# Local attention of the last sub-layer, rebuilt on four tiles per pass with one PSUM region for each function

## The chip, the core and the metric

The kernel runs on one core of a Trainium2 chip. The metric is the device time of one launch in microseconds (us), from the first to the last instruction and what little lies around it. Five engines work side by side, each through a list of its own in order: PE (matrix multiply, with its weight loads shown as PEld), DVE (VectorE), ACT (ScalarE), POOL (GpSimd) and SP (which issues DMAs). They wait for each other by semaphores only.

## The reference

Eight sub-layers are added to `x` (128 sequences of 64 tokens, width 128) one after another. The last one has two layers, each with a local attention (the part that is changed) and a gated GELU block. For one layer of the attention, with 8 heads of 64 and a window of 64 over sequences of 64 tokens (so one causal block for each sequence):

```python
h = shift_token(x)                      # second half of the columns comes from the token before
q, k, v = split(h @ wqkv)               # 8 heads of 64 each
q = l2norm(q) * qs ; k = l2norm(k) * ksc
q = q * cos * scale + rotate_half(q) * sin * scale
k = k * cos / scale + rotate_half(k) * sin / scale
attn = softmax(8.0 * q @ k.T  + causal mask)
x = x + (attn @ v) @ wo
```

## The kernel before

All of the program is a chain of stages, and every stage ends with a barrier of all engines. `X` and, in the last sub-layer, `y` (`l3f_y`) stay in SBUF: 64 tiles of 128 rows, where a tile holds two sequences of 64 tokens. `local_attention` runs twice (stages `la0`, `la1`), each time over the 64 tiles, as a software pipeline: the helper `steps` writes two steps (tile j = 0, 1) into the body of a loop, and `at(it, j, lag, work)` puts a function on the tile that lies `lag` tiles ahead. Within an engine the order is the order of the `at` lines; between engines only semaphores count. Every buffer exists twice (j).

PSUM has four regions of two banks each: `m.A[0]`, `m.A[1]`, `m.B[0]`, `m.B[1]`. Tile j uses `A[j]` (banks `F0`, `F1`) for h, q, k, v and the turned q and k, and `B[j]` (banks `G0`, `G1`) for scores, turned probabilities, mixed values and the projection.

The steps of one tile, with the lines of the profile:

- ACT copies the rows (L1942), PE turns them and shifts by a token with the `shift` matrix (`turn_y`, L2107 and L2108), ACT copies hT (L1947, L1949).
- PE makes q and k (`make_qk`, L2115, L2116), ACT squares them out of PSUM (L1955, L1956), DVE sums per head (`lengths`, L2003) and floors (L2006).
- POOL raises the sums to the power -0.5 (L2089). DVE multiplies q and k by it out of PSUM (`normalize`, L2012). POOL makes the two sine halves (L2095, L2096), DVE the cosine part (`cosines`, L2020), POOL adds them (L2099) into `la_qk`.
- PE makes v in the banks that q and k leave (`make_v`, L2121), ACT keeps v spread out with zeros (`values`, L1925); PE turns `la_qk` (`turn_qk`, L2130), and ACT and DVE copy q and k out, k spread out with zeros (L1967, L1930).
- PE makes the scores of 8 heads with a mask matmul (L2135) and 8 matmuls of 64x128 (`scores`, L2141); DVE takes the maxima and subtracts (`shift`, L2031, L2034); ACT takes the exponential (L1972); PE turns (L2151), ACT copies (L1977), PE mixes with v and a column of ones (`mix`, L2160), DVE divides (`outputs`, L2043, L2048), PE turns (L2168), ACT copies (L1982), PE projects (`project`, L2174), DVE adds to y (`add`, L2056).

Of the kernel before, what the change touches and what calls it, by code (L numbers as in the profile page):

```python
# [16 lines left out]
S = 64  # L17
# [1866 lines left out]

def local_attention(nc, m, d, y, layer):
# [3 lines left out]
    with Stage(nc, f"la{layer}") as st:  # L1889
# [4 lines left out]
        half_power = st.sb("half_power", [P, 2 * HEADS3])  # L1894
# [3 lines left out]
        ys, hT, hT2 = st.two("ys", [P, P]), st.two("hT", [P, P]), st.two("hT2", [P, 2, 2, S])  # L1898
        sq, qk, turned = (st.two(n, [P, 2, INNER]) for n in ("sq", "qk", "turned"))
        length, rlen = st.two("length", [P, 2 * HEADS3]), st.two("rlen", [P, 2 * HEADS3])  # L1900
        qT = st.two("qT", [P, G, P])
        kd = st.two("kd", [P, G, 2, 2, S])
        vd = st.two("vd", [P, 2, G, 2, W3 + 1])
        prob, pT = st.two("prob", [P, HEADS3, S]), st.two("pT", [P, G, P])
        top, inv = st.two("top", [P, HEADS3]), st.two("inv", [P, HEADS3])
        o, oT = st.two("o", [P, INNER]), st.two("oT", [P, G, P])
        loaded, ready, ones_set = st.sem("loaded"), st.sem("ready"), st.sem("ones_set")
        (y_copied, y_turned, h_copied, qk_made, squared, summed, floored, rooted, scaled, v_made, v_kept,
         cosed, sined, rotated, qk_turned, q_copied, k_kept_low, k_kept_high, scored, max_done,
         shifted, exped, p_turned, p_copied, mixed, inverted, o_done, o_turned, o_copied, out_done, added) = (  # L1910
            st.sem2(n) for n in ("y_copied", "y_turned", "h_copied", "qk_made", "squared", "summed", "floored",
                                 "rooted", "scaled", "v_made", "v_kept", "cosed", "sined",
                                 "rotated", "qk_turned", "q_copied", "k_kept_low", "k_kept_high", "scored",
                                 "max_done", "shifted", "exped", "p_turned", "p_copied", "mixed", "inverted",
                                 "o_done", "o_turned", "o_copied", "out_done", "added"))

        F0, F1 = [x[:, 0:CH] for x in m.A], [x[:, CH:2 * CH] for x in m.A]
        G0, G1 = [x[:, 0:CH] for x in m.B], [x[:, CH:2 * CH] for x in m.B]
        blocks = lambda x: x.rearrange("p (g q) -> p g q", g=G)

        def keep_v(eng_copy, j, u):

            r = slice(u * S, u * S + S)
            for b, src in enumerate((F0[j], F1[j])):
                last = eng_copy(vd[j][r, b, :, u, 0:W3], src.rearrange("p (g u w) -> p g u w", g=G, u=2)[r, :, u])  # L1925
            return last

        def keep_k(eng_copy, j, u):
            r = slice(u * S, u * S + S)
            return eng_copy(kd[j][r, :, :, u], F1[j].rearrange("p (g b k) -> p g b k", g=G, b=2)[r])  # L1930

        with nc.Block() as block:
# [4 lines left out]

            @block.scalar
            def _(act):
                def copy_y(it, j):  # L1940
                    act.wait_ge(y_turned[j], past(it))
                    act.copy(ys[j][:], y[:, it * 2 + j, :]).then_inc(y_copied[j], 1)  # L1942

                def copy_h(it, j):
                    act.wait_ge(y_turned[j], past(it + 1))
                    act.wait_ge(v_made[j], past(it))
                    act.copy(hT[j][:], F0[j][:, 0:P])  # L1947
                    for b in range(2):
                        last = act.copy(hT2[j][:, b], repeat_heads(F0[j][:, b * S:b * S + S], 2))  # L1949
                    last.then_inc(h_copied[j], 1)  # L1950

                def squares(it, j):
                    act.wait_ge(qk_made[j], past(it + 1))
                    act.wait_ge(rotated[j], past(it))
                    act.activation(sq[j][:, 0], F0[j], ACT.Square)  # L1955
                    act.activation(sq[j][:, 1], F1[j], ACT.Square).then_inc(squared[j], 1)  # L1956

                def values(it, j):
                    act.wait_ge(v_made[j], past(it + 1))
                    act.wait_ge(mixed[j], past(it))  # L1960
                    keep_v(act.copy, j, 0)
                    keep_v(act.copy, j, 1).then_inc(v_kept[j], 1)

                def copy_qk(it, j):
                    act.wait_ge(qk_turned[j], past(it + 1))
                    act.wait_ge(scored[j], past(it))
                    act.copy(qT[j][:], blocks(F0[j])).then_inc(q_copied[j], 1)  # L1967
                    keep_k(act.copy, j, 1).then_inc(k_kept_high[j], 1)

                def exps(it, j):  # L1970
                    act.wait_ge(shifted[j], past(it + 1))
                    act.activation(prob[j][:], prob[j][:], ACT.Exp, scale=8.0).then_inc(exped[j], 1)  # L1972

                def copy_p(it, j):
                    act.wait_ge(p_turned[j], past(it + 1))
                    act.wait_ge(mixed[j], past(it))
                    act.copy(pT[j][:], blocks(G1[j])).then_inc(p_copied[j], 1)  # L1977
# [17 lines left out]

                steps(act, step)

            @block.vector
            def _(dve):
                def lengths(it, j):  # L2000
                    dve.wait_ge(squared[j], past(it + 1))
                    dve.wait_ge(rooted[j], past(it))
                    dve.tensor_reduce(length[j][:], sq[j][:].rearrange("p n (h w) -> p (n h) w", h=HEADS3), AX,  # L2003
                                      ALU.add).then_inc(summed[j], 1)
                    dve.wait_ge(summed[j], past(it + 1))
                    dve.tensor_scalar(length[j][:], length[j][:], 1e-24, None, ALU.max).then_inc(floored[j], 1)  # L2006

                def normalize(it, j):
                    dve.wait_ge(rooted[j], past(it + 1))
                    dve.wait_ge(qk_turned[j], past(it))  # L2010
# [547 lines left out]
```

## Time and profile before

| | us |
|---|---|
| median of three runs | 5108.8 (5107.85 to 5109.19) |
| profiled execution, its own time | 5109.92 |
| its span, first to last instruction | 5108.1 |
| PE busy over the span | 4115.2 (81%) |
| DVE busy | 3229.7 (63%) |
| ACT busy | 2027.8 (40%) |
| POOL busy | 1890.4 (37%) |

The two attention stages are two of some twenty stages. Each of them goes through 64 tiles at an even pace, so they are best read as one tile's pace times 64 plus what the beginning and the end take. In the rows below, a line of the timeline gives the start, the duration (of a merged group: from the first start to the last end), the engine, the line, the operation with output and inputs, how many records it has, and in brackets how long the engine had been idle and what released it. A group line of the profile gives the busy time, the mean of one instruction in ns, and the idle time before. An fp32 matmul shows two records, a transpose one.

### The profile page before, as it was taken

Reading aid. Unit: us, or ns where it says so; the run is one execution under the profiler, and the core shown is the slowest. Engines: PE = TensorE matmul, PEld = TensorE weight load, DVE = VectorE, ACT = ScalarE, POOL = GpSimd, SP = SyncE. Lnnn points to the kernel's source line nnn. Section 1 sums busy time; section 2 is a strip of 40 time slices with the busy share of each in tenths; the row PEclk is TensorE's granted clock in tenths of the full one; section 3 lists DMA queues with packets and bytes.
Section 4 is the critical chain, followed back from the end, with each engine's and each line's share of the span. In section 5 each row is a group of like instructions: output and inputs, shape, how many; then the busy total and the mean of one; then the engine's idle time right before and its main releaser. Section 6 shows DMA issues by size and latency. Waiting matters only on the chain. (4 is left out here: it accounts for less than half of the span.)

```text
span 5108.1 us, 83277 instructions
## 1 busy us (share of the span) xinstructions
PE 4115.2 (81%) x25803; PEld 2577.4 (50%) x25803; DVE 3229.7 (63%) x6921; ACT 2027.8 (40%) x4429; POOL 1890.4 (37%) x1457
## 2 busy tenths in 40 slices
PE   6772899998995850469959979699898889989987
PEld 5441444445773320346646656355555445555544
DVE  3998301106776698857767755577776447777744
ACT  1332222224663154334422236455555225555521
POOL 0775000002330054135510000288887018888810
PEclk9996899999996975789959975699999989999999
DMA  2110000000000000021100020000000000000000
GB/s 75 41 40 13 23 0 0 0 0 13 11 11 7 0 0 0 0 60 35 35 14 0 0 75 8 11 0 0 0 0 0 5 11 0 0 0 0 0 5 33
DMA packets 76953, 67.34 MB, mean 13 GB/s; under 512 B 11988, under 2 KB 72536, under 8 KB 75736
## 3 DMA queue, kind: packets, MB, share of 16 engines
q1 hardware_dynamic: 75448, 66.23, 4.3%
q8 instruction: 29, 0.48, 0.0%
q10 hardware_dynamic: 1440, 0.34, 0.0%
q14 instruction: 36, 0.29, 0.0%
HBM read 62.34 MB, written 4.19 MB: 13 GB/s over the span
## 5 line engine op out<-in xcount | busy, mean ns | idle before, releaser
L2089 POOL TENSOR_TENSOR la_rlen<-la_length,la_half_power 128x16 f32<-128x16 f32 x128 | 372.8, 2912 | 55.6 <-DVE la_length L2006 48.8
L2099 POOL TENSOR_TENSOR la_qk<-la_turned,la_sq 128x1024 f32<-128x1024 f32 x128 | 301.2, 2353 | 46.7 <-DVE la_turned L2020 39.2
L750 DVE TENSOR_TENSOR l0f_y<-A,l0f_s 128x512 f32<-128x512 f32 x16 | 11.1, 692 | 463.4 <-PE A L717 463.4
L2096 POOL TENSOR_TENSOR la_sq<-la_qk,la_sin 128x512 f32<-128x512 f32 x128 | 259.7, 2029 | 0.0
L2121 PE MATMUL A<-la_wv,la_hT 128*128 128x512 f32 x512 | 257.3, 625 | 1.4 <-DVE la_qk L2012 1.4
L2012 DVE TENSOR_TENSOR la_qk<-A,la_rlen 128x512 f32<-128x512 f32 x256 | 164.9, 687 | 145.2 <-POOL la_rlen L2089 145.2
L1925 ACT COPY la_vd<-A 64x256 f32<-64x256 f32 x512 | 163.6, 369 | 228.5 <-PE A L2121 227.1
L2130 PE MATMUL A<-ident,la_qk 128*128 128x128 f32 x1024 | 137.3, 277 | 136.1 <-ACT la_vd L1925 87.2
L2082 POOL COPY la_vd<-half 128x8 f32<-128x8 f32 x8 | 1.2, 198 | 657.1 <-POOLq L47 657.1
L1006 POOL COPY l1x_vd<-half 128x16 f32<-128x16 f32 x4 | 0.6, 213 | 650.6 <-POOLq L47 650.6
L1869 PE MATMUL A<-l1f_wT,l1f_down_oq 128*128 128x128 f32 x384 | 54.2, 307 | 226.0 <-DVE l1f_down_oq L1830 225.9
L2095 POOL TENSOR_TENSOR la_sq<-la_qk,la_sin 128x512 f32<-128x512 f32 x128 | 163.8, 1280 | 179.4 <-DVE la_qk L2012 179.4
L1015 POOL TENSOR_TENSOR l1x_kx<-l1x_kT,head_of 128x512 f32<-128x512 f32 x128 | 130.8, 1043 | 263.2 <-ACT l1x_kT L1116 263.2
L2130 PEld LDWEIGHTS A<-ident,la_qk 128*128 128x128 f32 x1024 | 110.4, 141 | 166.8 <-POOL la_qk L2099 164.5
L1972 ACT ACTIVATE la_prob<-la_prob 128x512 f32<-128x512 f32 x128 | 81.0, 633 | 285.7 <-DVE la_prob L2034 285.7
L2020 DVE TENSOR_TENSOR la_turned<-la_qk,la_cos 128x1024 f32<-128x1024 f32 x128 | 189.4, 1479 | 0.1
L1930 DVE COPY la_kd<-A 64x512 f32<-64x512 f32 x128 | 87.4, 683 | 150.8 <-PE A L2130 150.8
L2303 ACT ACTIVATE gg_gate<-B,gg_b 128x512 f32<-128x512 f32 (+1 forms) x96 | 65.9, 686 | 280.0 <-PE B L2334 280.0
L1869 PEld LDWEIGHTS A<-l1f_wT,l1f_down_oq 128*128 128x128 f32 x384 | 51.3, 218 | 230.2 <-DVE l1f_down_oq L1830 215.1
L2003 DVE TENSOR_REDUCE la_length<-la_sq 128x16 f32<-128x1024 f32 x128 | 154.8, 1209 | 14.3 <-ACT la_sq L1956 14.3
L2160 PEld LDWEIGHTS B<-la_vd,la_pT 128*64 128x64 f32 x2048 | 111.1, 136 | 92.8 <-issue 92.5
L2291 POOL TENSOR_TENSOR gg_rstd<-gg_var,gg_half_power 128x4 f32<-128x4 f32 x32 | 32.3, 1009 | 335.5 <-DVE gg_var L2248 335.5
(442 smaller groups left out, 11947.5 us busy)
## 6 DMA issues: line engine op xcount, KB each, us to landing
memory_ctx<-in_ctx SPq DMA_DIRECT2D x128, 64.0 KB, 2.2
l2x_ctx<-in_ctx SPq DMA_DIRECT2D x128, 64.0 KB, 2.2
X<-in_x SPq DMA_DIRECT2D x4, 1024.0 KB, 8.7
gates_ctxT<-in_ctxT SPq DMA_DIRECT2D x16, 256.0 KB, 2.7
memory_ctxT<-in_ctxT SPq DMA_DIRECT2D x64, 64.0 KB, 1.7
l1x_ctxT<-in_ctxT SPq DMA_DIRECT2D x64, 64.0 KB, 1.7
l2x_raw<-in_l2x_mask SPq DMA_DIRECT2D x2, 2048.0 KB
l2x_ctxT<-in_ctxT SPq DMA_DIRECT2D x64, 64.0 KB, 1.7
```

Of the source, the lines that this page charges most:

```text
L1015: last = pool.tensor_tensor(kx[j][:, b], repeat_heads(k_in[j][:, b * S:b * S + S], E), spread_heads(m.head_of_8[:], S), ALU.mult)
L1925: last = eng_copy(vd[j][r, b, :, u, 0:W3], src.rearrange("p (g u w) -> p g u w", g=G, u=2)[r, :, u])
L2003: dve.tensor_reduce(length[j][:], sq[j][:].rearrange("p n (h w) -> p (n h) w", h=HEADS3), AX, ALU.add).then_inc(summed[j], 1)
L2012: last = dve.tensor_tensor(per_head(qk[j][:, n], HEADS3, W3), per_head(src, HEADS3, W3), spread_heads(rlen[j][:, n * HEADS3:(n + 1) * HEAD ...
L2020: dve.tensor_tensor(heads(turned[j][:]), heads(qk[j][:]), cos[:, :, None, :].broadcast_to([P, 2, HEADS3, W3]), ALU.mult)\
L2089: pool.tensor_tensor(rlen[j][:], length[j][:], half_power[:], ALU.pow).then_inc(rooted[j], 1)
L2095: pool.tensor_tensor(z[:, :, :, lo], x[:, :, :, hi], along(lo), ALU.mult)
L2096: pool.tensor_tensor(z[:, :, :, hi], x[:, :, :, lo], along(hi), ALU.mult).then_inc(sined[j], 1)
L2099: pool.tensor_tensor(qk[j][:], turned[j][:], sq[j][:], ALU.add).then_inc(rotated[j], 1)
L2121: last = pe.matmul(dst, hT2[j][:, b].rearrange("p u k -> p (u k)"), wv[:], start=True, stop=True)
L2130: last = pe.transpose(dst[:, g * P:g * P + P], qk[j][:, n, g * P:g * P + P], m.ident[:])
L2160: last = pe.matmul(dst[b * S:b * S + S, g % 2 * n:g % 2 * n + n], pT[j][:, g, b * S:b * S + S], vd[j][:, b, g].rearrange("p u w -> p (u w) ...
```

## The change

`local_attention` is written anew. The rest of the program is the same.

- Four tiles per loop body instead of two (`steps4`, `at4`), one counting semaphore for each event (`done(it, j, back)` is the count at which tile `it*4+j-back` has done it).
- PSUM regions by function, each used by every tile in turn: `made` (q and k), `keyed` (turned q and k; then turned h in its upper bank and v in its lower one), `tried` (scores and turned probabilities), `used` (mixed values; then turned outputs and projection).
- The shifted rows come by DMA from `y` into `hs` (three DMAs a tile, issued by SP), and one transpose turns them (`turn_h`).
- q and k are not normalized first: DVE multiplies the raw q and k out of PSUM by cosine and sine (`cosines`, `sine_terms`), POOL adds (`rotate`) and then scales by the inverse length (`scale`).
- The inverse length is Exp(-0.5 * Ln(65536 * length)) on ACT (`root`) instead of a power on POOL; the factor is undone by 256 in the tables. POOL floors the sums (`floor`).
- Scores, mix and v use tiles of 64 columns: 16 matmuls of 64x64 for the scores, 16 of 64x65 for the mix, 4 of 64x256 for v. The copies with zeros between (`kd`, `vd`) go.
- q and k are copied in one ACT copy of 1024 columns, v in one of 512, the squares are one ACTIVATE of 1024.

The core of the diff (old parts of `local_attention` that only fall away are in the listing above):

```diff
+def at4(it, j, lag, work, quads=QUADS):
+    quad, j = it + (j + lag) // 4, (j + lag) % 4
...
+        made, keyed, tried, used = m.A[0], m.A[1], m.B[0], m.B[1]
+        sim = banks(tried)[:, :, 0:G * S].rearrange("p u (g k) -> p u g k", g=G)
+        turned_p = banks(tried)[:, :, G * S:CH]
+        turned_o, projected = used[:, 0:CH], used[:, CH:CH + P]
+        turned_h, made_v = keyed[:, CH:CH + P], keyed[:, 0:CH]
...
+                def shift_in(it, j):
+                    sp.wait_ge(h_turned, done(it, j, 4))
+                    sp.dma_start(hs[j][:, 0:S], y[:, t, 0:S]).then_inc(h_in[j], 16)
+                    for b in range(0, P, S):
+                        sp.dma_start(hs[j][b + 1:b + S, S:P], y[b:b + S - 1, t, S:P]).then_inc(h_in[j], 16)
...
             @block.scalar
+                def copy_qk(it, j):
+                    act.wait_ge(qk_turned, done(it, j))
+                    act.wait_ge(scored, done(it, j, 2))
+                    act.copy(qkT[j % 2][:].rearrange("p n g q -> p (n g q)"), keyed[:]).then_inc(qk_copied, 1)
+                def root(it, j):
+                    act.wait_ge(floored, done(it, j))
+                    act.wait_ge(scaled_qk, done(it, j, 2))
+                    act.activation(rlen[j % 2][:], length[j % 2][:], ACT.Ln, scale=65536.0).then_inc(logged, 1)
+                    act.wait_ge(logged, done(it, j))
+                    act.activation(rlen[j % 2][:], rlen[j % 2][:], ACT.Exp, scale=-0.5).then_inc(rooted, 1)
...
+                def values(it, j):
+                    act.wait_ge(v_made, done(it, j))
...
-                    at(it, j, 2, copy_y)
-                    at(it, j, 0, copy_qk)
-                    at(it, j, -1, copy_p)
-                    at(it, j, 2, copy_h)
-                    at(it, j, 0, exps)
-                    at(it, j, 2, squares)
-                    at(it, j, 1, values)
-                    at(it, j, -1, copy_o)
+                    at4(it, j, 0, copy_qk)
+                    at4(it, j, -1, copy_p)
+                    at4(it, j, -2, copy_o)
+                    at4(it, j, 0, exps)
+                    at4(it, j, 1, values)
+                    at4(it, j, 3, squares)
+                    at4(it, j, 4, copy_h)
+                    at4(it, j, 2, root)
             @block.vector
+                    at4(it, j, 2, cosines)
+                    at4(it, j, 2, sine_terms)
+                    at4(it, j, 0, shift)
+                    at4(it, j, 2, lengths)
+                    at4(it, j, -2, add)
+                    at4(it, j, -1, outputs)
             @block.gpsimd
+                    at4(it, j, 1, scale)
+                    at4(it, j, 2, rotate)
+                    at4(it, j, 2, floor)
             @block.tensor
+                def turn_qk(it, j):
+                    pe.wait_ge(scaled_qk, done(it, j))
+                    pe.wait_ge(v_kept, done(it, j))
+                    pe.wait_ge(h_copied, done(it, j, -3) if not isinstance(it, int) else min(done(it, j, -3), NT + BEFORE))
+                def scores(it, j):
+                    pe.wait_ge(p_copied, done(it, j, 1))
+                    pe.matmul(banks(tried)[:, 0, 0:G * S], m.ident_bf[:], repeat_heads(m.causal_bf[:], G),
+                              start=True, stop=False)
+                    pe.wait_ge(qk_copied, done(it, j))
+                    pe.matmul(banks(tried)[:, 1, 0:G * S], m.ident_bf[:], repeat_heads(m.causal_bf[:], G),
+                              start=True, stop=False)
+                    for g in range(G):
+                        for b in range(2):
+                            for u in range(2):
+                                r, c = slice(u * S, u * S + S), slice(b * S, b * S + S)
+                                last = pe.matmul(sim[c, u, g], qkT[j % 2][r, 0, g, c], qkT[j % 2][r, 1, g, c],
+                                                 start=False, stop=(g == G - 1))
+                def make_v(it, j):
+                    pe.wait_ge(qk_copied, done(it, j, 1))
```

The order of the instructions on two engines in the loop bodies. ACT before, the first of the two tiles of the body: `la_qT` and the first `la_kd` are the turned q and k, `la_sq` the squares.

```order
L1942 COPY la_ys<-l3f_y 128x128
L1967 COPY la_qT<-A 128x512
L1930 COPY la_kd<-A 64x8x64
L1977 COPY la_pT<-B 128x512
L1945 REGISTER_ALU
L1947 COPY la_hT<-A 128x128
L1949 COPY la_hT<-A 128x128 x2
L1972 ACTIVATE la_prob<-la_prob 128x512
L1955 ACTIVATE la_sq<-A 128x512
L1956 ACTIVATE la_sq<-A 128x512
L1925 COPY la_vd<-A 64x4x64 x4
L1982 COPY la_oT<-B 128x512
```

There is no table load in the loop. ACT in the changed kernel, from the copy of h (`la_hT`) through `root` (`la_rlen`) to the values of the next step:

```order
L2015 COPY la_hT<-A 128x128
L1986 REGISTER_ALU
L1988 ACT_TABLE_LOAD
L1988 ACTIVATE la_rlen<-la_length 128x16
L1990 ACT_TABLE_LOAD
L1990 ACTIVATE la_rlen<-la_rlen 128x16
L1982 REGISTER_ALU
L1983 COPY la_qkT<-A 128x1024
L1995 COPY la_pT<-B 128x512
L2000 COPY la_oT<-B 128x512
L2004 ACTIVATE la_prob<-la_prob 128x512
L2009 COPY la_vd<-A 128x8x64
```

The logarithm (L1988) and the exponential (L1990) of `root` have each got a table load, eight in the body of four tiles, and the copies of a tile stand behind them.

PE before, one tile of the body (`A` and `B` are the PSUM regions, `la_wv` the weights of v):

```order
L2130 MATMUL A<-ident,la_qk 128x128 x8
L2151 MATMUL B<-ident,la_prob 128x128 x4
L2174 MATMUL B<-la_wo,la_oT 128x128 x4
L2107 MATMUL A<-ident,la_ys 64x128
L2108 MATMUL A<-shift,la_ys 64x128
L2135 MATMUL B<-causal_bf,ident_bf 128x512
L2141 MATMUL B<-la_kd,la_qT 64x128 x8
L2115 MATMUL A<-la_wq,la_hT 128x512
L2116 MATMUL A<-la_wk,la_hT 128x512
L2160 MATMUL B<-la_vd,la_pT 64x130 x8
L2121 MATMUL A<-la_wv,la_hT 128x512 x2
L2168 MATMUL B<-ident,la_o 128x128 x4
```

PE in the changed kernel, from the masks of a tile's scores to the end of its step:

```order
L2160 MATMUL B<-causal_bf,ident_bf 128x256
L2163 MATMUL B<-causal_bf,ident_bf 128x256
L2169 MATMUL B<-la_qkT 64x64 x16
L2153 REGISTER_ALU
L2154 REGISTER_ALU
L2155 MATMUL A<-la_wq,la_hT 128x512
L2156 MATMUL A<-la_wk,la_hT 128x512
L2176 MATMUL B<-la_wo,la_oT 128x128 x4
L2181 REGISTER_ALU
L2182 MATMUL A<-ident,la_hs 128x128
L2188 MATMUL A<-la_wv,la_hT 64x256 x4
L2203 MATMUL B<-la_vd,la_pT 64x65 x16
```

The matmuls of v (L2188) now stand behind the scores (L2169), q and k of a later tile (L2155, L2156) and the projection (L2176); before, they stood behind the mix, and waited for the normalized q and k.

On POOL the power (L2089) and both sine halves (L2095, L2096) are gone, the sum stays, and the scaling (1024 columns) and the floor (16 columns) are new.

## Rows read from the trace of the kernel before

**Rows 1.** Busy time in stretches: us, PE, PEld, DVE, ACT, POOL (records), clock, DMA share.

```profile
3600.00:3809.00 209.00, 188.63 (x1382) 121.58 (x1381) 157.18 (x260) 118.58 (x301) 170.68 (x81) 1.00 0.00 0
150.00:200.00 50.00, 38.56 (x417) 24.09 (x416) 45.55 (x104) 16.22 (x42) 39.75 (x52) 1.00 0.15 41
3100.00:3150.00 50.00, 45.85 (x195) 32.13 (x194) 30.05 (x131) 32.46 (x132) 0.00 (x0) 0.50 0.00 0
```

**Rows 2.** Timeline of one tile of la0 on POOL and DVE; the last row: a tile later.

```profile
3598.80 2.92 POOL L2089 TENSOR_TENSOR la_rlen<-la_length,la_half_power 128x16 f32<-128x16 f32 x1
...
3601.75 1.29 DVE L2012 TENSOR_TENSOR la_qk<-A,la_rlen 128x512 f32<-128x512 f32 x2 [1.05 <-POOL la_rlen L2089]
...
3603.11 1.26 POOL L2095 TENSOR_TENSOR la_sq<-la_qk,la_sin 128x512 f32<-128x512 f32 x1 [1.40 <-DVE la_qk L2012]
...
3604.33 2.32 POOL L2096 TENSOR_TENSOR la_sq<-la_qk,la_sin 128x512 f32<-128x512 f32 x1
...
3606.73 2.35 POOL L2099 TENSOR_TENSOR la_qk<-la_turned,la_sq 128x1024 f32<-128x1024 f32 x1
...
3609.28 2.91 POOL L2089 TENSOR_TENSOR la_rlen<-la_length,la_half_power 128x16 f32<-128x16 f32 x1 [0.19 <-DVE la_length L2006]
```

**Rows 3.** The same timeline, the maxima of two tiles that follow each other.

```profile
3602.98 0.69 DVE L2031 TENSOR_REDUCE la_top<-B 128x8 f32<-128x512 f32 x1
...
3613.43 0.69 DVE L2031 TENSOR_REDUCE la_top<-B 128x8 f32<-128x512 f32 x1
```

**Rows 4.** The same timeline: PE from the projection of a tile to the values.

```profile
3600.16 1.06 PE L2174 MATMUL B<-la_wo,la_oT 128*128 128x128 f32 x8
...
3601.52 0.39 PE L2135 MATMUL B<-causal_bf,ident_bf 128*128 128x512 bf16 x1
...
3601.84 1.09 PE L2141 MATMUL B<-la_kd,la_qT 128*64 128x128 f32 x16
...
3602.86 1.12 PE L2115 MATMUL A<-la_wq,la_hT 128*128 128x512 f32 x2
...
3605.82 1.98 PE L2121 MATMUL A<-la_wv,la_hT 128*128 128x512 f32 x4
...
3607.64 0.60 PE L2168 MATMUL B<-ident,la_o 128*128 128x128 f32 x4
...
3607.84 1.29 ACT L1925 COPY la_vd<-A 64x256 f32<-64x256 f32 x4 [1.80 <-PE A L2121]
...
3609.27 1.06 PE L2130 MATMUL A<-ident,la_qk 128*128 128x128 f32 x8 [1.03 <-ACT la_vd L1925]
```

**Rows 5.** Groups of instructions on ACT: busy us, mean ns of one, idle before.

```profile
L1137 ACT COPY l1x_pT<-A 128x1024 f32<-128x1024 f32 x64 | 64.8, 1012 | 39.4 <-PE A L1197 39.4
L1972 ACT ACTIVATE la_prob<-la_prob 128x512 f32<-128x512 f32 x128 | 81.0, 633 | 285.7 <-DVE la_prob L2034 285.7
L1956 ACT ACTIVATE la_sq<-A 128x512 f32<-128x512 f32 x128 | 75.4, 589 | 0.0
L1977 ACT COPY la_pT<-B 128x512 f32<-128x512 f32 x128 | 75.0, 586 | 3.1
L1947 ACT COPY la_hT<-A 128x128 f32<-128x128 f32 x128 | 34.1, 266 | 15.4 <-PE A L2108 15.4
L409 ACT ACTIVATE memory_low<-memory_low 128x8 f32<-128x8 f32 x64 | 12.8, 200 | 0.6
```

**Rows 6.** Timeline of ACT where an exponential and a logarithm follow each other.

```profile
103.86 0.63 ACT L290 ACTIVATE decay_l<-decay_f 128x512 f32<-128x512 f32 x1
104.51 1.28 ACT L292 ACT_TABLE_LOAD   x1
105.80 0.63 ACT L292 ACTIVATE decay_l<-decay_l 128x512 f32<-128x512 f32 x1
```

**Rows 7.** Timeline of PE in the l2x stage, 64-column tiles with 18 moving columns.

```profile
2500.99 1.11 PE L1208 MATMUL B<-l2x_vd,l2x_pT 128*64 128x18 f32 x32 [0.16 <-ACT l2x_pT L1137]
```

**Rows 8.** Groups of instructions on DVE, same columns as Rows 5.

```profile
L1051 DVE TENSOR_TENSOR l1x_prob<-A,l1x_top 128x1024 f32<-128x1024 f32 x64 | 78.4, 1225 | 2.2
L2003 DVE TENSOR_REDUCE la_length<-la_sq 128x16 f32<-128x1024 f32 x128 | 154.8, 1209 | 14.3 <-ACT la_sq L1956 14.3
```

**Rows 9.** Timeline of PE at the start of la1.

```profile
4180.72 0.47 PE L2107 MATMUL A<-ident,la_ys 128*64 128x128 f32 x1 [12.46 <-DMA la_by_swapped<-in_l3f_scale_swapped]
...
4182.12 2.08 PE L2115 MATMUL A<-la_wq,la_hT 128*128 128x512 f32 x2 [0.70 <-ACT la_hT L1949]
```

**Rows 10.** The adds to y in both layers: duration min/median/max, first and last start.

```profile
L2056 DVE TENSOR_TENSOR l3f_y<-l3f_y,B x128: 272/275/289, 3316.4 to 4873.2; 128x128 f32 x120, 128x128 f32<-128x128 f32 x8
```

More of the change, by code:

```diff
@@ L1882, with done, steps4 @@
 PARTS3 = [(n, min(P, HID3 - n)) for n in range(0, HID3, P)]
+QUADS = NT // 4
+BEFORE = 4
+def done(it, j, back=0):
+    return it * 4 + j + 1 + BEFORE - back
+def at4(it, j, lag, work, quads=QUADS):
+    quad, j = it + (j + lag) // 4, (j + lag) % 4
+    if not isinstance(quad, int) or 0 <= quad < quads:
+        work(quad, j)
+def steps4(eng, step, quads=QUADS):
+    for it in (-1, 0):
+        for j in range(4):
+            step(it, j)
+    with eng.Fori(1, quads - 1) as it:
+        for j in range(4):
+            step(it, j)
+    for it in (quads - 1, quads):
+        for j in range(4):
+            step(it, j)
 def local_attention(nc, m, d, y, layer):
@@ L1917, in local_attention @@
[L1917 to L1930, printed above, removed]
+        qkT = st.two("qkT", [P, 2, G, P])
@@ L1938, in _ @@
+                steps4(sp, step)
             @block.scalar
             def _(act):
-                def copy_y(it, j):
-                    act.wait_ge(y_turned[j], past(it))
-                    act.copy(ys[j][:], y[:, it * 2 + j, :]).then_inc(y_copied[j], 1)
-                def copy_h(it, j):
[L1945 to L1950, printed above, removed]
@@ L1964, in copy_qk @@
[L1964 to L1977, printed above, removed]
@@ L1998, in _ @@
+                    at4(it, j, 2, root)
+                steps4(act, step)
             @block.vector
             def _(dve):
-                def lengths(it, j):
[L2001 to L2006, printed above, removed]
@@ L2053, in add, with cosines @@
-                def add(it, j):
-                    t = it * 2 + j
-                    dve.wait_ge(out_done[j], past(it + 1))
-                    dve.tensor_tensor(y[:, t, :], y[:, t, :], G1[j][:, 0:P], ALU.add).then_inc(added[j], 1)
-                for j in range(2):
-                    dve.memset(kd[j][:], 0.0).then_inc(ones_set, 1)
-                    dve.memset(vd[j][:, :, :, :, 0:W3], 0.0).then_inc(ones_set, 1)
+                def cosines(it, j):
+                    dve.wait_ge(squared, done(it, j))
+                    dve.wait_ge(scaled_qk, done(it, j, 2))
+                    dve.tensor_tensor(heads(turned[j % 2][:]), made_heads,
+                                      cos[:, :, None, :].broadcast_to([P, 2, HEADS3, W3]), ALU.mult)\
+                       .then_inc(cosed, 1)
@@ new lines, in turn_p, with turn_o @@
+                def turn_p(it, j):
+                    pe.wait_ge(exped, done(it, j))
+                    for g in range(G):
+                        last = pe.transpose(turned_p[:, g // 2, g % 2 * P:g % 2 * P + P],
+                                            prob[j % 2][:, g].rearrange("p u k -> p (u k)"), m.ident[:])
+                    last.then_inc(p_turned, 1)
+                def turn_o(it, j):
+                    pe.wait_ge(o_done, done(it, j))
+                    for g in range(G):
+                        last = pe.transpose(turned_o[:, g * P:g * P + P], o[j % 2][:, g * P:g * P + P], m.ident[:])
+                    last.then_inc(o_turned, 1)
@@ new lines, in scores, with project, turn_h @@
+                    last.then_inc(scored, 1)
+                def project(it, j):
+                    pe.wait_ge(o_copied, done(it, j))
+                    for g in range(G):
+                        last = pe.matmul(projected, oT[j % 2][:, g], wo[:, g], start=(g == 0), stop=(g == G - 1))
+                    last.then_inc(out_done, 1)
+                def turn_h(it, j):
+                    pe.wait_ge(h_in[j], it * 48 + 48)
+                    pe.wait_ge(qk_copied, done(it, j, 4))
+                    pe.transpose(turned_h, hs[j][:], m.ident[:]).then_inc(h_turned, 1)
@@ L2177, in _ @@
+                    last.then_inc(mixed, 1)
                 pe.wait_ge(loaded, 16 * len(loads))
```

297 lines of the change are left out of this document (131 added, 166 removed).

## The prediction

> **What bounds the kernel now.** I read the stretches first [rows 1]: in steady attention (3600 to 3809 us) PE is busy 90%, POOL 82%, DVE 75%, ACT 57%, at a granted clock of 1.00 (2.4 GHz). None is full, so a loop through several engines sets the pace. The timeline shows it [rows 2]: power 2.92 on POOL, then `normalize` on DVE 1.29 (POOL idle for 1.40), the sine halves 1.26 and 2.32, the sum 2.35, a gap of 0.19, and the next power. Together 10.4, and the maxima of two tiles lie 10.45 us apart [rows 3]. That is the pace P of before; 64 tiles in each of two layers make 1338 us. The rest of the program is the same, so each us of P is worth 128 us.
>
> **What goes.** The whole POOL loop. DVE now needs nothing from POOL to read q and k, and POOL has two passes of 1024 columns at 2.35 and a floor of 16 columns: bounded below by about 0.2 and above by the power's 2.9 [rows 2], so 4.9 to 7.6 a tile. DVE: cosines out of PSUM 1.23 and sums 1.21 (1024 columns, [rows 8]), the sine halves 2 x 0.65 as `normalize` [rows 2], maxima 0.69 [rows 3], the subtraction as much, some 1.1 for division and add: 6.2. Neither sets a pace near 10.
>
> **What comes: one loop through ACT and PE.** The table of the order decides here. In a step ACT does copy q and k of t, copy p of t-1, copy o of t-2, exponential of t, values of t+1, squares of t+3, h of t+4, root of t+2. The values of t+1 wait for `make_v` of t+1, which on PE stands behind the scores of t, q and k of t+3, the projection of t-2 and the turned h. The scores of t wait for the copy of p of t-1, since `tried` exists once. So nothing of this overlaps within a tile's pace, and I add it up from the start of copy_qk (running sum in brackets):
>
> - ACT: copy of 1024 columns 1.01 and of 512 columns 0.59 [rows 5], and 0.02 behind each (1.62).
> - ACT to PE 0.14: the values' copy ends at 3609.13, the transpose starts at 3609.27 [rows 4] (1.76).
> - Masks to the first score 0.32 as before: 3601.52 to 3601.84; 512 bf16 columns stay 512 (2.08).
> - Scores: 16 matmuls, 32 records. Before, 16 records of 128 moving columns took 1.02 to the start of the next group, of which 0.86 is eight pairs at 0.107 and 0.16 the way out [rows 4]. With few columns a record of a 64-column tile takes (1.11 - 0.21) / 31 = 0.029, a pair 0.058 [rows 7]; that is 0.93 for 16 pairs, 0.46 if four go together, 1.70 if the two row halves go one after another (32 x 0.053). No row shows tiles of 64 rows. I take 0.60, nearer to four together, since the row halves write different banks and share nothing; with the way out 0.76 (2.84).
> - q and k of t+3: four records of 512 columns, as the values' four from 3605.82 to 3607.64: 1.82 (4.66).
> - Projection: eight records at (1.06 - 0.275) / 7 = 0.112: 0.90 (5.56). Turned h: 0.11 (5.67).
> - Values: 0.10 for the change of tile size, then eight records of 256 columns in four pairs, 0.213 each (half of 0.427), the last ending 0.17 later and the first 0.05 slower: 1.07 (6.84). If the pairs do not overlap, 0.85 more.
> - PE to ACT 0.04; the copy of v 0.59, squares 0.589 + 512 x 0.833 ns = 1.02, h 0.27 [rows 5], 0.02 behind each (8.82).
> - Root: two table loads at 1.283 (1.28 in [rows 6]), two ACTIVATEs of 16 columns at 0.20 (128x8, [rows 5]), four times 0.02: 3.05 (11.87).
>
> Then copy_qk of the next tile starts: its transposes wait only for h (at 8.82), take PE 0.14 + 1.03, and are there at 10.0; those of p at 10.6. So they are hidden, by 1.2 us; without the table loads they would be next, and the gain from leaving these out would end near 1.4.
>
> What lies beside this loop: the subtraction of t ends near 4.4 and the exponential near 5.1, both before the values at 6.88. POOL scales t+1 from 0 and is done with the sum near 4.9; the sums of DVE come near 5.6, the floor by 6.0 to 8.7, needed at 8.8 at the earliest. The DMAs of h run up to four tiles ahead, some 45 us, and cost PE no wait; if that cover went, a wait of a few us would stand in front of the turned h. The copies with zeros and the copies of y cost nothing before either (they lay in ACT's idle 43%), so their going brings nothing. I take the mix, 16 of 64x65, at the scores' 0.76; it stands behind the values in PE's idle time.
>
> So P goes from 10.45 to 11.87. The bounds: scores at 0.46 and no extra for tile sizes (0.26 less) 11.47; scores at 1.70 12.97. Beginning and end of a layer take 24 us before (4180.7 to 4873.5 less 64 x 10.45, [rows 9, 10]), partly at half clock (q's two records 2.08 instead of 1.12, [rows 4, 9]). Two more tiles in flight add some, fewer semaphores to set at the start take a little: +6, between -5 and +15. **Sum:** 2 x (64 x 1.42 + 6) = 194. Against the profiled execution's own 5109.9 (span 5108.1 and 1.8 around it; 1.1 over the median) that is 5304.
>
> **Two pages weighed against the rows.** Where an exponential is followed by a logarithm in the trace, the load starts 0.02 after the ACTIVATE ends and the next ACTIVATE 0.01 after the load [rows 6]: a switch costs 1.29. The Trainium skill ("ScalarE: Activation LUTs", What ACT_TABLE_LOAD costs) gives 1283 ns for the load plus about 1380 ns of drain at each switch; the trace shows no such drain, and by that rule P would be an estimated 2.76 longer (14.63, 5657). The Trainium skill, same page, section "Table sets: the hidden batching unit", says that exponential and logarithm share a set and need one load; by this an estimated 1.3 would fall away, 5137, but the program as built has both loads in the loop body, so this gets no chance. The Trainium skill, "TensorEngine Tiling (Array Packing)", Key Properties, says that different tiles run weight loads and matmuls in parallel, and that a change of the tiling mode drains TensorE. The drain agrees with the rows (0.10 to 0.16 at each change, [rows 4]); on four tiles at once no run here speaks, and by this rule alone the scores would be 0.46, P 11.73 and the time 5286.
>
> **The rivals.**
> - *The loop does not close, and the busiest engine sets the pace (faster).* This would need PE to have `make_v` done before ACT wants it. ACT's own sum is 1.03 + 0.61 + 0.61 + 0.65 + 0.61 + 1.04 + 0.29 + 3.05 = 7.89, and 3.98 of P is idle before exponential and values. The sign turns where this idle time is below 10.45 - 7.89 = 2.56. At nothing, P is 7.9 and the time 5110 - 2 x (64 x 2.55 - 6) = 4796. For it: PE's whole work is some 7.5. Against: both queues are in order, and the wait of the scores for the copies is in the same step.
> - *The row halves go one after another.* P 12.97, 5445.
> - *The clock falls.* PE's share falls from 90% to some 65%. At half clock (1.2 GHz) the PE part of the loop (1.76 to 6.84) adds 5.1: P 17, near 5960. For it: the l3x stage ran throughout at 0.50. Against: the memory stage, with PE busy 77%, kept 1.00 [rows 1].
> - *Each load empties ACT first.* If ACT stood idle at each load for as long as the load itself takes (1.28), P would be 11.87 + 2.57 = 14.44 and the time 5110 + 2 x (64 x 3.99 + 6) = 5633. Against: the 0.02 and 0.01 around the load in [rows 6].
> - *Nothing changes.* The new loop would happen to be 10.3 to 10.4 long.
>
> **The chances.** The forecast has 0.73, serial row halves 0.08, half clock 0.08, drains 0.04, the faster case 0.05, no change 0.02. The likeliest is 5304. The range takes the bounds of the scores, the tile changes and the ends: low 2 x (64 x 1.02 - 5) above 5110, that is 5230, opened to 5220; high the serial case with the ends at +15, 5463. It leaves out half clock, drains and the faster cases, some 0.19. A measurement here can tell 0.2% (10 us) from no change: faster 0.05, same 0.02, slower 0.93.
>
> **What would show it.** Maxima (DVE) 11.9 us apart; two table loads of 1283 ns for each tile, 256 in all; ACT idle about 2.2 before the exponential (released by DVE) and 1.8 before the values (released by PE); PE idle before the scores some 3 us a tile, released by ACT; DVE and POOL far from full, POOL's passes 2.35 or less; clock 1.00. The step on the scores is read off as the distance from the first score to the next q: 0.76. I am wrong if ACT does not wait for the values, if the pace is set by DVE or POOL, or if the clock is below 1.00 in the steady part.

## The result, and the profile after

| | before | after |
|---|---|---|
| median of four runs, us | 5108.96 (5107.85 to 5109.19) | 5302.32 (5301.92 to 5303.88) |
| span of the profiled execution | 5108.1 | 5300.5 |
| mean granted clock of TensorE | 0.899 | 0.883 |
| from first to last maxima, la0 and la1 | 659.2 and 659.4 | 752.1 and 752.1 |

The ratio is 1.0379, with a 95% interval of 1.0362 to 1.0397: the changed kernel is slower by 3.8%. The forecast was 5304, in a range from 5220 to 5463.

The page of the profile shows which engines wait. Its group lines give the busy time, the mean of one in ns, and the idle time before. These are of the changed kernel:

```profile
L2105 POOL TENSOR_TENSOR la_scaled<-la_turned,la_rlen 128x1024 f32<-128x1024 f32 x128 | 243.4, 1902 | 844.7 <-ACT la_rlen L1990 844.7
L2059 DVE TENSOR_REDUCE la_top<-B 128x8 f32<-128x512 f32 x128 | 88.6, 692 | 413.4 <-PE B L2169 413.4
...
L2160 PE MATMUL B<-causal_bf,ident_bf 128*128 128x256 bf16 x128 | 36.4, 284 | 310.9 <-ACT la_pT L1995 310.9
...
L2009 ACT COPY la_vd<-A 128x512 f32<-128x512 f32 x128 | 75.1, 587 | 339.1 <-PE A L2188 339.1
L2155 PE MATMUL A<-la_wq,la_hT 128*128 128x512 f32 x256 | 194.8, 852 | 14.8 <-DVE la_sines L2049 14.0
...
L2004 ACT ACTIVATE la_prob<-la_prob 128x512 f32<-128x512 f32 x128 | 80.8, 631 | 278.5 <-DVE la_prob L2062 278.5
...
L1990 ACT ACT_TABLE_LOAD x128 | 164.2, 1283 | 2.3
L1988 ACT ACT_TABLE_LOAD x128 | 164.2, 1283 | 2.2
```

POOL waits 6.6 us a tile (844.7 / 128) for the inverse length of ACT, where it had 1.6 us idle before [rows 2]. A tile, ACT waits 2.6 us for the values of PE (1.8 in the tile below, 3.5 in the tile ahead of it, where the clock falls) and 2.2 for the subtraction of DVE, and PE waits 2.4 for the turned probabilities that ACT copies. The two engines wait for each other, as a loop through both would have it. ACT idles 0.02 us before a load (2.3 / 128).

The timeline of one tile, from the copy of q and k to the next one, ACT, PE and the maxima (rows of DVE and POOL beside it and the weight loads are left out):

```profile
3675.41 0.99 ACT L1983 COPY la_qkT<-A 128x1024 f32<-128x1024 f32 x1
...
3676.30 0.59 ACT L1995 COPY la_pT<-B 128x512 f32<-128x512 f32 x1
...
3676.94 0.28 PE L2160 MATMUL B<-causal_bf,ident_bf 128*128 128x256 bf16 x1 [2.48 <-ACT la_pT L1995]
...
3677.26 0.69 PE L2169 MATMUL B<-la_qkT 64*64 64x64 f32 x32
...
3677.89 1.13 PE L2155 MATMUL A<-la_wq,la_hT 128*128 128x512 f32 x2
...
3678.03 0.69 DVE L2059 TENSOR_REDUCE la_top<-B 128x8 f32<-128x512 f32 x1 [3.20 <-PE B L2169]
...
3679.71 1.05 PE L2176 MATMUL B<-la_wo,la_oT 128*128 128x128 f32 x8
...
3680.60 0.27 PE L2182 MATMUL A<-ident,la_hs 128*128 128x128 f32 x1
3680.80 1.08 PE L2188 MATMUL A<-la_wv,la_hT 128*64 128x256 f32 x8
...
3682.01 0.59 ACT L2009 COPY la_vd<-A 128x512 f32<-128x512 f32 x1 [1.81 <-PE A L2188]
3682.49 1.03 ACT L2020 ACTIVATE la_sq<-A 128x1024 f32<-128x1024 f32 x1
...
3683.41 0.27 ACT L2015 COPY la_hT<-A 128x128 f32<-128x128 f32 x1
...
3683.70 1.28 ACT L1988 ACT_TABLE_LOAD   x1
...
3684.99 0.22 ACT L1988 ACTIVATE la_rlen<-la_length 128x16 f32<-128x16 f32 x1
...
3685.22 1.28 ACT L1990 ACT_TABLE_LOAD   x1
...
3686.52 0.22 ACT L1990 ACTIVATE la_rlen<-la_rlen 128x16 f32<-128x16 f32 x1
3686.64 0.99 ACT L1983 COPY la_qkT<-A 128x1024 f32<-128x1024 f32 x1
```

The loop is the one of the sum, and it takes 11.23 us here. The tile ahead of it is longer, though it has the same instructions. Its rows on PE and DVE:

```profile
3664.10 0.28 PE L2160 MATMUL B<-causal_bf,ident_bf 128*128 128x256 bf16 x1 [2.48 <-ACT la_pT L1995]
...
3664.42 0.69 PE L2169 MATMUL B<-la_qkT 64*64 64x64 f32 x32
...
3665.05 2.07 PE L2155 MATMUL A<-la_wq,la_hT 128*128 128x512 f32 x2
...
3665.18 0.69 DVE L2059 TENSOR_REDUCE la_top<-B 128x8 f32<-128x512 f32 x1 [3.20 <-PE B L2169]
...
3666.91 1.80 PE L2156 MATMUL A<-la_wk,la_hT 128*128 128x512 f32 x2
...
3668.55 1.05 PE L2176 MATMUL B<-la_wo,la_oT 128*128 128x128 f32 x8
```

And the stretches of both tiles, with the columns of [rows 1] (the granted clock is the number behind POOL's):

```profile
3661.00:3664.00 3.00, 0.62 (x6) 0.38 (x4) 0.98 (x2) 2.97 (x6) 1.18 (x1) 1.00 0.00 0
3664.00:3668.00 4.00, 3.90 (x38) 2.08 (x39) 2.51 (x3) 1.16 (x3) 3.10 (x3) 0.63 0.00 0
...
3674.00:3677.00 3.00, 0.52 (x6) 0.28 (x5) 0.82 (x2) 2.99 (x5) 1.34 (x1) 1.00 0.00 0
3677.00:3681.00 4.00, 4.00 (x49) 2.60 (x51) 2.58 (x4) 1.01 (x2) 3.02 (x3) 1.00 0.00 0
```

In both tiles PE takes up work at the 2.4 GHz level after an idle stretch of 2.48 us. In the first the granted clock is then at 1.2 GHz from 3665.05, where q begins, to 3668.46; in the next it stays at 2.4. Such a piece at 1.2 GHz is called a fall from here on. From the first score to the projection that is 4.13 us or 2.45 us: a fall costs 1.68. The maxima lie 12.85 apart (3665.18 to 3678.03) behind a fall and 11.2 without one. The mean of the steady tiles is 12.09, so some 55% of them have a fall: (12.09 - 11.16) / 1.68. Counted, 32 of the 63 distances in each layer are above 12.

The span can be split by the maxima (engine, operation, count: shortest/median/longest in ns, first to last start; before la0 and la1, then after la0 and la1):

```profile
L2031 DVE TENSOR_REDUCE la_top<-B x64: 681/692/693, 3289.6 to 3948.8; 128x8 f32<-128x512 f32 x64
...
L2031 DVE TENSOR_REDUCE la_top<-B x64: 681/691/693, 4204.2 to 4863.6; 128x8 f32<-128x512 f32 x64
```

```profile
L2059 DVE TENSOR_REDUCE la_top<-B x64: 691/692/693, 3293.9 to 4046.0; 128x8 f32<-128x512 f32 x64
...
L2059 DVE TENSOR_REDUCE la_top<-B x64: 691/692/693, 4304.0 to 5056.1; 128x8 f32<-128x512 f32 x64
```

The first maxima come 4.3 us later, 92.9 are lost in la0, 2.6 between the layers, 92.7 in la1, and -0.1 behind them. That is 192.4, all of the span's difference.

### The profile page after: what moved, and what is told of

Its sections match the earlier page's. It is cut to its first block and busy times, and to the rows that moved or that the text cites. A ratio compares the mean times of both kernels' runs of the same rounds, so it can differ in the third digit from the quotient of the medians.

```text
span 5300.5 us, 91807 instructions
## 1 busy us (share of the span) xinstructions
PE 3981.3 (75%) x30155; PEld 2513.7 (47%) x30155; DVE 3001.3 (57%) x6417; ACT 2184.9 (41%) x3915; POOL 1361.6 (26%) x1319
## 5 line engine op out<-in xcount | busy, mean ns | idle before, releaser
L2111 POOL TENSOR_TENSOR la_turned<-la_turned,la_sines 128x1024 f32<-128x1024 f32 x128 | 300.8, 2350 | 692.3 <-DVE la_sines L2049 692.3
L2105 POOL TENSOR_TENSOR la_scaled<-la_turned,la_rlen 128x1024 f32<-128x1024 f32 x128 | 243.4, 1902 | 844.7 <-ACT la_rlen L1990 844.7
L2059 DVE TENSOR_REDUCE la_top<-B 128x8 f32<-128x512 f32 x128 | 88.6, 692 | 413.4 <-PE B L2169 413.4
L2135 PE MATMUL A<-ident,la_scaled 128*128 128x128 f32 x1024 | 139.4, 279 | 145.4 <-ACT la_hT L2015 145.0
L2009 ACT COPY la_vd<-A 128x512 f32<-128x512 f32 x128 | 75.1, 587 | 339.1 <-PE A L2188 339.1
L2155 PE MATMUL A<-la_wq,la_hT 128*128 128x512 f32 x256 | 194.8, 852 | 14.8 <-DVE la_sines L2049 14.0
L2176 PEld LDWEIGHTS B<-la_wo,la_oT 128*128 128x128 f32 x1024 | 159.1, 221 | 93.7 <-issue 89.6
L2156 PE MATMUL A<-la_wk,la_hT 128*128 128x512 f32 x256 | 190.5, 838 | 0.0
L2135 PEld LDWEIGHTS A<-ident,la_scaled 128*128 128x128 f32 x1024 | 109.7, 141 | 164.0 <-ACT la_hT L2015 145.6
L2041 DVE TENSOR_TENSOR la_turned<-A,la_cos 128x1024 f32<-128x1024 f32 x128 | 156.8, 1225 | 44.0 <-ACT la_sq L2020 26.7
```

What stands on the lines that cost most here:

```text
L2041: dve.tensor_tensor(heads(turned[j % 2][:]), made_heads, cos[:, :, None, :].broadcast_to([P, 2, HEADS3, W3]), ALU.mult)\
L2105: pool.tensor_tensor(by_head(scaled), by_head(turned), spread_heads(rlen[j % 2][:], W3), ALU.mult)\
L2111: pool.tensor_tensor(turned[j % 2][:], turned[j % 2][:], sines[j % 2][:], ALU.add)\
L2135: last = pe.transpose(keyed[:, n * CH + g * P:n * CH + g * P + P], scaled[j % 2][:, n, g * P:g * P + P], m.ident[:])
L2155: pe.matmul(made[:, 0:CH], hT[j][:], wq[:], start=True, stop=True)
L2156: pe.matmul(made[:, CH:2 * CH], hT[j][:], wk[:], start=True, stop=True).then_inc(qk_made, 1)
```

## The experiments

Two theories stood against each other on the size. **A**, the loop: what lies on the path from `copy_qk` through the scores, q and k, the projection, v, and ACT's copies and root sets the pace, and each piece of it counts in full. **B**, the clock: the pace is set in good part by the falls that follow PE's idle stretch. Rivals on the cause were the root's loads alone, and the new tile forms. The loads have runs of their own below; the tile forms are read from the timeline alone, and no run undid them, the DMAs of h or the new PSUM regions. All ratios are to the kernel before, timed anew beside the runs (5109.89 for the first four, 5108.59 for the last four).

**The root back on POOL.** ACT's logarithm and exponential go, POOL has the power again, and the 256 in the tables goes.

```diff
-                    at4(it, j, 2, root)
...
+                def power(it, j):
...
+                    pool.tensor_tensor(rlen[j % 2][:], length[j % 2][:], half_power[:], ALU.pow).then_inc(rooted, 1)
...
                     at4(it, j, 2, floor)
+                    at4(it, j, 2, power)
```

> The changed kernel, with one part undone: the inverse length is again a power on POOL (as before, 16 columns), so ACT has neither the logarithm and the exponential of root nor their two table loads. Theory (one loop through ACT and PE, with root at its end, sets the pace): root's 2.95 us leave the loop, and the next thing to be waited for is PE's transposes of q, k and p that stood hidden behind root; the pace goes from 11.16 to about 9.7 us a tile at full clock, 128 tiles save 1.5 each and the time is near 5110, or near 4990 if the clock's dips go too. POOL holds 2.35 + 1.90 + 2.92 + 0.2 = 7.4 a tile and does not bind. Rival (the table loads are hidden behind PE, and PE's own work with its dips sets the pace): the time stays at 5302 within 0.5%.

Measured: 4970.03 (4967.07 to 4972.62), ratio 0.9726 (0.971 to 0.9743). This one edit turns the loss of 3.8% into a gain of 2.7%. The timeline where the root stood:

```profile
3646.23 0.27 ACT L2009 COPY la_hT<-A 128x128 f32<-128x128 f32 x1
...
3646.55 1.09 PE L2137 MATMUL A<-ident,la_scaled 128*128 128x128 f32 x8 [1.15 <-ACT la_hT L2009]
...
3647.68 1.02 ACT L1984 COPY la_qkT<-A 128x1024 f32<-128x1024 f32 x1 [1.18 <-PE A L2137]
...
3649.24 0.28 PE L2162 MATMUL B<-causal_bf,ident_bf 128*128 128x256 bf16 x1 [0.72 <-ACT la_pT L1989]
```

```profile
3600.00:3700.00 100.00, 80.13 (x1087) 55.62 (x1086) 65.17 (x96) 45.54 (x74) 77.60 (x42) 1.00 0.03 7
```

From the end of the copy of h to `copy_qk` 1.18 us pass, where the root took 2.96 (3683.68 to 3686.64): the transposes that it hid are next. That takes 1.8 of 11.2, and 9.4 is what the maxima show (3640.92 to 3650.32; the mean of the steady tiles is 9.46). PE's idle stretch ahead of the masks shrinks to 0.72 to 0.79, and the clock is 1.00 in the steady tiles. So the root, two loads and two short ACTIVATEs, cost both, its own time and the falls: 332 us in all, of which about 1.8 x 128 = 230 are the loop.

**v right behind the scores.** One line of the order moves on PE.

```diff
                     at4(it, j, 0, scores)
+                    at4(it, j, 1, make_v)
                     at4(it, j, 3, make_qk)
                     at4(it, j, -2, project)
                     at4(it, j, 4, turn_h)
-                    at4(it, j, 1, make_v)
```

> The changed kernel with one line of PE's order moved: make_v stands right behind the scores, ahead of q and k, projection and turned h. Same work on every engine. Theory (ACT waits for v, because v stands last in PE's queue): ACT's idle 1.8 us before the copy of v goes, squares are then what waits for PE; the pace goes from 11.16 to about 9.7 at full clock, the time to about 5110 (4990 if the clock's dips go). Rival (ACT's chain from the exponential on, or a loop that does not hold v, sets the pace): no change, 5302 within 0.5%.

Measured: 5067.97 (5060.35 to 5068.22), ratio 0.9915 (0.9898 to 0.9931). The wait of ACT for the values is gone, and a tile without a fall takes 9.74 to 9.82:

```profile
3650.68 0.69 DVE L2059 TENSOR_REDUCE la_top<-B 128x8 f32<-128x512 f32 x1 [1.44 <-PE B L2169]
...
3652.67 0.57 ACT L2009 COPY la_vd<-A 128x512 f32<-128x512 f32 x1
...
3653.58 1.02 ACT L2020 ACTIVATE la_sq<-A 128x1024 f32<-128x1024 f32 x1 [0.34 <-PE A L2156]
...
3660.43 0.69 DVE L2059 TENSOR_REDUCE la_top<-B 128x8 f32<-128x512 f32 x1 [1.42 <-PE B L2169]
```

So the place of `make_v` closes the loop, as A has it. (The pace that comes next is 9.74, far from the 7.9 of ACT's own work.) Now ACT waits a little for k (L2156) ahead of the squares, and for the exponential. Tiles with a fall remain (11.16 in the one ahead, 3639.52 to 3650.68; clock 0.96 from 3600 to 3700).

**More work on PE, in its idle stretch.** To tell B apart, the turn of o is written five times: 16 transposes more a tile, on PE alone, that nobody needs.

```diff
-                    for g in range(G):
+                    for g in [g for _ in range(5) for g in range(G)]:
```

> The changed kernel with work added: PE turns the outputs o five times over instead of once (the same 4 transposes into the same PSUM, 16 more a tile, 1.74 us), in the gap of 2.5 us in which it waits for ACT before the scores. Theory on the clock (tiles of 12.84 us alternate with tiles of 11.16 because the granted clock falls to half in PE's idle gap and rises again some us into the scores' and q's matmuls): with the gap filled the clock stays at 1.00, every tile takes 11.16, and the time falls by up to 128 x 0.93 = 119 us, to about 5190, though work is added. Rival (the alternation comes from a beat between the engines' queues, the clock only follows): the time stays at 5302 or rises by what does not fit, up to 30 us.

Measured: 5200.65 (5199.7 to 5201.84), ratio 1.018 (1.0163 to 1.0197). Work was added, and 102 us went. The timeline and the stretch:

```profile
3646.76 2.35 PE L2149 MATMUL B<-ident,la_o 128*128 128x128 f32 x20
...
3649.84 0.28 PE L2160 MATMUL B<-causal_bf,ident_bf 128*128 128x256 bf16 x1 [0.73 <-ACT la_pT L1995]
```

```profile
3600.00:3700.00 100.00, 83.43 (x1071) 62.83 (x1071) 54.68 (x80) 63.90 (x99) 39.70 (x27) 1.00 0.03 6
```

ACT and PE go through the same loop, the distances are 11.16 to 11.24 in every steady tile, and none has a fall. So the falls cost some 102 us of the changed kernel's time, and the other 91 (5200.65 - 5109.89) are the loop at full clock. The shares are not exact: between the first and the last maxima of the layers 110 us go (55.4 and 54.4), and 8 come back between the layers and behind them.

**Two loads more.** ACT does a logarithm and an exponential of ones ahead of the root, so four loads a tile.

```diff
+                    act.activation(spare[:], ones[:], ACT.Ln)
+                    act.activation(spare[:], ones[:], ACT.Exp)
                     act.activation(rlen[j % 2][:], length[j % 2][:], ACT.Ln, scale=65536.0).then_inc(logged, 1)
```

> The changed kernel with the suspected cost doubled: ahead of root's own logarithm and exponential stand another logarithm and exponential of 16 columns (into spare buffers), with two more table loads, four a tile. Theory (root is on the loop, each load costs its 1.28 and no more): the pace rises by root's 2.95, 128 x 2.95 = 378 us, to about 5680; if each switch drained ACT in addition it would be 700 or more; if root were hidden, 5302.

Measured: 5924.13 (5923.02 to 5925.23), ratio 1.1596 (1.1572 to 1.1619), which is 244 more than the 5680 that were expected. A tile takes 17.05:

```profile
3642.19 1.28 ACT L1993 ACT_TABLE_LOAD   x1
...
3643.71 1.28 ACT L1994 ACT_TABLE_LOAD   x1
3645.01 0.21 ACT L1994 ACTIVATE la_rlen<-la_length 128x16 f32<-128x16 f32 x1
3645.24 1.28 ACT L1996 ACT_TABLE_LOAD   x1
...
3648.19 0.39 PE L2167 MATMUL B<-causal_bf,ident_bf 128*128 128x256 bf16 x1 [5.54 <-ACT la_pT L2001]
```

```profile
3648.00:3655.50 7.50, 7.31 (x53) 4.40 (x55) 2.79 (x4) 1.26 (x3) 3.32 (x3) 0.59 0.00 0
```

The added pair costs its 3.0 us (the loads start 1.52 apart), and no drain: the ACTIVATE starts 0.02 behind the load, and the load 0.02 behind the ACTIVATE. The rest of the 17.05, some 2.8, is the clock: PE idles 5.54, the masks take 0.39 instead of 0.28, every tile has a fall, and from the first mask to the turned h 6.47 us pass (3648.19 to 3654.66) where the tile at full clock took 3.66 (3676.94 to 3680.60). The Trainium skill ("ScalarE: Activation LUTs", What ACT_TABLE_LOAD costs) has a drain of about 1380 ns at each switch; no row here shows one.

**Both first edits.** The root on POOL and v behind the scores.

> Both single edits together: the power back on POOL (no table loads) and make_v right behind the scores. Theory (both waits, ACT's for v and the copies' behind root, lie on one loop; with both gone PE's queue and DVE are nearly full and set the pace): about 8.8 us a tile at clock 1.00, 128 x (8.8 - 9.46) below the 4970 of the power alone, near 4885. Rival (with root gone the wait for v is no longer on the loop): 4970 stays.

Measured: 4891.73 (4890.0 to 4895.02), ratio 0.9578 (0.9562 to 0.9594), a tile 8.78, the clock 1.00. The two gains are 332 and 234 alone and 411 together, 155 less than their sum. The falls, gone wholly in one run and in part in the other, can go only once; that explains no more than some 100 to 120 of it. The rest was not taken apart: PE is now busy 86% and POOL 83% from 3600 to 3700.

**The loads apart.** The exponential of the root moves behind the exponential of the scores in the next step. There are still two loads a tile.

```diff
+                def root_exp(it, j):
...
                     at4(it, j, 0, exps)
+                    at4(it, j, 1, root_exp)
                     at4(it, j, 1, values)
```

> The changed kernel with root cut in two: the logarithm stays at the end of ACT's step, the exponential of the inverse length moves behind the softmax exponential of the next step. Still two table loads a tile, but the second now stands in front of the softmax exponential, where ACT waits 2.1 us for DVE anyway. Theory (what costs is where the loads stand, not that they are there): about 1.3 to 1.5 us of the loop go; a new loop opens (exponential of the inverse length, POOL's scaling, transposes, copies, scores, maxima), 10.0 to 10.4 us long, so the time is 5140 to 5190 at the full clock, and the clock's dips become fewer since PE's gap shrinks. Rival (each load costs its time wherever it stands): 5302.

Measured: 5018.28 (5014.57 to 5020.31), ratio 0.9824 (0.9807 to 0.984). The gain is larger than forecast. The timeline on ACT:

```profile
3651.09 1.28 ACT L2006 ACT_TABLE_LOAD   x1
...
3653.27 0.63 ACT L2006 ACTIVATE la_prob<-la_prob 128x512 f32<-128x512 f32 x1 [0.89 <-DVE la_prob L2065]
```

One load of the two lies now in ACT's wait for the subtraction, which shrinks from 2.19 to 0.89. The steady tiles take 9.63 to 9.91, 9.74 in the mean, all at clock 1.00: PE's idle stretch ahead of the masks is 0.95 to 1.23. The loop is the old one less one load and one short ACTIVATE (11.2 less 1.5); the loop through POOL and the scores, expected at 10.0 to 10.4, must be shorter than expected, since the pace is 9.74. So it is the place of a load on the loop that costs, not its being there.

**The loads apart, and v behind the scores.** The edits of the second and the sixth run together.

> Root cut in two and make_v behind the scores. Theory: the loop that is left after the cut goes through POOL's scaling and the scores, and v is not on it, so moving v brings nothing more: the same time as with root cut alone, within 0.5%. Rival (v is always on the loop): another 1 us a tile, some 130 us less.

Measured: 5024.87 (5023.72 to 5026.02), ratio 0.9837 (0.9817 to 0.9857), the same as without the move of v. Here ACT waits for POOL's floor ahead of the logarithm:

```profile
3653.05 0.21 ACT L1988 ACTIVATE la_rlen<-la_length 128x16 f32<-128x16 f32 x1 [1.44 <-POOL la_length L2120]
```

The wait for v is gone, and one of 1.44 stands in its place. So v was not off the path, as was expected: with the loads apart ACT still waited 1.6 to 1.7 for it. But a second loop, of the inverse length, POOL's passes and its floor, was just as long: in the sixth run the floor ended at 3648.95 and the logarithm began at 3648.99. Opening one of two loops of the same length brings nothing.

**The best of these.** The fifth run, and p ahead of q and k, in the turns on PE and the copies on ACT.

```diff
+                    at4(it, j, -1, copy_p)
                     at4(it, j, 0, copy_qk)
-                    at4(it, j, -1, copy_p)
```

> Power on POOL, make_v behind the scores, and in addition the turning and the copying of p of t-1 stand ahead of those of q and k of t, on PE and on ACT, since the scores wait for the copy of p. Theory (copying p, 0.5 us, leaves the way from the transposes to the scores, but the transposes of q and k start 0.4 later): about 0.15 us a tile less than without it, near 4865. Rival (no difference): 4885.

Measured: 4862.41 (4862.13 to 4862.86), ratio 0.9519 (0.9503 to 0.9535): 4.8% faster than the kernel before and 8.3% faster than the changed one. That is 29 us less than the fifth run, 0.2 a tile, near the 0.15 that was expected. A tile takes 8.5 to 8.7 (from 3600 to 3700 POOL is busy 86%, PE 88%, and the clock is 1.00).

## Why the prediction was right

The loop is the one named, and its parts came out close. That the time, 5302.3, lies only 2 us from the forecast is luck, for three errors cancel: over the 128 tiles the loop at full clock was put some 90 us too long (11.87 for 11.16) and the ends 30 too long, and the falls of the clock, some 119 (128 x 0.93), were left out. From the timeline of the tile at full clock:

- **ACT's first copies.** Forecast 1.62, measured 1.48 (3675.41 to 3676.89). The sum put 0.02 between instructions; in fact the next one starts about 0.1 before the end that the record shows (3676.30 against 3676.40). The same between the copy of v and the squares (0.48 for 0.61) and the squares and h (0.92 for 1.04).
- **ACT to PE.** 0.05 instead of 0.14 (3676.89 to 3676.94).
- **Masks.** 0.32, as forecast.
- **Scores.** 0.63 from the first score to q, forecast 0.76, bounds 0.62 to 1.86. This is what four tiles at once would give (0.46 and the way out of 0.16), so the rival of serial row halves is out. It is also what the Trainium skill ("TensorEngine Tiling (Array Packing)", Key Properties) has, that different tiles run weight loads and matmuls in parallel.
- **q, k, projection.** 1.82 and 0.89, forecast 1.82 and 0.90.
- **h and values.** 0.20 and 1.21, forecast 0.11 and 1.07 with 0.10 for the change of tile form and 0.04 to ACT: 1.41 against 1.32.
- **ACT behind the values.** 1.69 to the load (3682.01 to 3683.70), forecast 1.94.
- **Root.** 2.94, forecast 3.05; each load 1.28, no drain. The rival of drains is out.

Together 11.2 at full clock for 11.87. Of the 0.6 to 0.7 too much some 0.5 is overlap on ACT between instructions that follow each other; the scores and the way from ACT to PE give 0.2, and h and the values take 0.1 of that back.

- **The clock.** The sum had it at 1.00, and half clock throughout was a rival at 0.08. Neither came: PE falls in about every second tile, for 3.4 us that lie over q and k in the tile shown, and that adds 0.93 to the mean (the run with more work on PE: 102 us). The step that failed is "Against: the memory stage, with PE busy 77%, kept 1.00": a busy share taken over a stretch does not tell how the idle time is cut up. In that stretch (150 to 200 us) PE was never idle for longer than 0.57 us at a time, in the changed kernel it is for 2.48 in each tile. The share was even forecast well (65%; 69% measured from 3600 to 3700).
- **Ends.** Forecast +6 a layer on top of 64 x 1.42, that is 97. Measured 96 a layer (192.4 / 2). With the steady distance of 12.09, 64 x 1.64 would be 105, so the ends take 9 less, not 6 more: with no work for later tiles behind it the loop shrinks in the last tiles.
- **Behind the loads.** The transposes of q and k were to be next once the loads go, with a gain that ends near 1.4. The first run shows that mechanism, with 1.8 (2.96 less 1.18). My own numbers gave it: the transposes of q and k were there at 10.0, 1.9 ahead of 11.87. The transposes of p, at 10.6, gave the 1.2 by which the prediction called them hidden, and nothing needs these before `copy_p`, one copy later; its 1.4 agrees with neither.
- **POOL.** Its passes take 1.90 and 2.35, the floor 0.20. It waits, as forecast, and is no bound.
- **The signs.** ACT idles 2.2 before the exponential (forecast 2.2) and 1.8 before the values (1.8), PE 2.5 before the masks (about 3). The maxima 11.9 apart are right only as the mean over all (752.1 / 63 = 11.94), and the clock of 1.00 was wrong: it is 0.93 from 3600 to 3700. By the prediction's own words ("I am wrong ... if the clock is below 1.00 in the steady part") this part of it failed.

The case in which the loop does not close was a rival at 0.05; the run with v moved shows that the place of one line opens this loop, though what comes next, 9.74, is well above the 7.9 of that rival.

## What to carry to other kernels

When work of one engine is moved to another, ask where it lands in that engine's order, and whether a second engine stands still behind it: two loads of 1.28 on ACT with their two short ACTIVATEs, on a path that PE waits for, cost 332 us of 5302, falls of the clock included; with one of the loads in a wait, 284 of these were back. Add up a loop from the order of both engines, and look for one instruction that closes it; a move of one line took 234 us out of it, and nothing where a second loop was as long. Where a change leaves PE with an idle stretch in each round, look at the length of that stretch and not only at the busy share (here 2.48 us came with falls in about half of the tiles), and test what the clock costs with work that nobody needs.

## What the runs showed of the hardware

- PE's idle stretch ahead of the masks and its granted clock from 3600 to 3700 us, over the runs: 0.7 to 0.8 us and 1.00 (root on POOL, more work on PE), 1.0 to 1.2 and 1.00 (loads apart), 1.5 to 1.8 and 0.96 to 0.97 (the two runs with v moved and both loads kept; with the loads apart 0.8 in some tiles), 2.5 and 0.93 (the changed kernel), 5.5 and 0.81 (four loads). In the changed kernel the fall comes once work has begun again (at 3665.05, the masks at 3664.10), and not in each round; with four loads the masks are slow already (0.39), in each round.
- 16 fp32 matmuls of 64x64 (32 records) took 0.63 us to the start of the next group, and 16 of 64x65 (the mix) 0.70 to their last end.
- A multiply of 128x1024 by a factor spread over 64 columns takes POOL 1.90 us, an add of the same size 2.35.
- Instructions that follow each other on ACT without a wait start some 0.1 us before the recorded end of the one ahead (3676.30 against 3676.40); behind and ahead of a table load it is 0.01 to 0.02 after it.
